# Chunked delta-rule layer on one core: an array cleared on GpSimd, and inverse and merge steps placed ahead of the convolution taps in VectorE's order

## The reference, cut to what matters

```
h = layernorm(x) * (1 + ca) + sa                      # ca, sa, ga: rows of silu(c) @ wmod
q, k = silu(conv4(h @ Wq)), silu(conv4(h @ Wk))       # conv4: causal, 4 taps along the sequence
v = silu(conv4(h @ Wv));  gate = h @ Wg
beta = sigmoid(h @ Wb);   g = -exp(A_log) * softplus(h @ Wa + dt_bias)
S = S * exp(g_t);  S = S + k_t (beta_t (v_t - k_t S));  o_t = q_t S      # for every t, k and q of length 1
x = x + ga * ((rmsnorm(o) * norm_weight * silu(gate)) @ Wo)
x = x + gb * ffn(layernorm(x) * (1 + cb) + sb)
```

## Time and profile before

| | us |
|---|---|
| median of 3 runs | 1088.68 |
| lowest, highest | 1088.04, 1089.65 |
| the profiled execution, its own time | 1088.38 |
| its span, first to last instruction | 1086.3 |
| PE busy | 1043.1 |
| DVE busy | 634.1 |
| ACT busy | 374.6 |
| POOL busy | 208.5 |

### The profile page before, as it was taken

How to read it: one execution, slowest core, us unless ns; L and a number is a source line. 1 busy time by engine, 2 the same in 40 slices (tenths; PEclk the granted TensorE clock), 3 DMA queues, 4 the chain that set the end, 5 groups by cost and what they waited for, 6 DMA issues and landing times.

```text
span 1086.3 us, 18632 instructions
## 1 busy us (share of the span) xinstructions
PE 1043.1 (96%) x7356; PEld 841.0 (77%) x7356; DVE 634.1 (58%) x995; ACT 374.6 (34%) x685; POOL 208.5 (19%) x163
## 2 busy tenths in 40 slices
PE   6999988999998999999899999999999999999998
PEld 4766666878776888888677887888888888888886
DVE  6877357989955777788756233342442433334356
ACT  4576465345446333344463113121121212122110
POOL 1312200011025445444321000000000000004191
PEclk8999998999999999999999999999999999999999
DMA  6505135837447466775630001010010100002223
GB/s 223 181 10 155 40 84 145 246 100 191 93 108 180 103 145 138 176 171 120 218 88 30 1 1 59 1 59 1 18 42 1 59 1 29 30 1 68 78 78 116
DMA packets 153430, 97.34 MB, mean 90 GB/s; under 512 B 93568, under 2 KB 130688, under 8 KB 153216
## 3 DMA queue, kind: packets, MB, share of 16 engines
q1 hardware_dynamic: 153344, 96.16, 32.3%
HBM read 64.67 MB, written 31.46 MB: 88 GB/s over the span
## 4 chain that ended last, share of the span: by engine, by line
PE 80%; DVE 9%; ACT 4%; issue 4%; SPq 1%; DMA 1%; POOL 0%; DVEq 0%; ACTq 0%
PE ps L1277 76%; ACT t L1600 3%; PE ps L1285 3%; DVE t L1976 3%; DVE t L1871 2%; DVE t L1876 1%; PE ps L1483 1%; DMA t<-in_x 1%; DVE t L2087 1%; DVE t L2076 1%; ACT L1622 1%; DVE t L1881 1%; SPq L1214 1%; DMA t<-scrU 0%; DVE t L2042 0%
## 5 line engine op out<-in xcount | busy, mean ns | idle before, releaser
L1277 PE MATMUL ps<-t,t 128*128 128x512 f32 (+6 forms) x6488 | 990.5, 336 | 33.7 <-DVE t L1871 12.2
L1277 PEld LDWEIGHTS ps<-t,t 128*128 128x128 f32 (+4 forms) x6488 | 783.5, 165 | 220.1 <-issue 42.4
L1871 DVE TENSOR_TENSOR t<-ps,t 128x512 f32<-128x512 f32 (+4 forms) x306 | 208.2, 701 | 254.9 <-PE ps L1277 240.2
L1600 ACT ACTIVATE t<-t 128x512 fp32r<-128x512 f32 (+10 forms) x339 | 189.0, 579 | 305.6 <-DVE t L1871 202.3
L1871 DVE TENSOR_TENSOR t<-t,t 128x512 fp32r<-128x512 f32 (+15 forms) x212 | 168.4, 799 | 109.3 <-ACT t L1600 104.9
L1600 ACT ACTIVATE t<-ps 128x512 f32<-128x512 f32 (+5 forms) x202 | 109.2, 552 | 321.0 <-PE ps L1277 309.2
L2355 POOL TENSOR_TENSOR t<-t,t 128x512 f32<-128x512 f32 x16 | 22.5, 1408 | 375.3 <-DVE t L1871 373.1
L1976 DVE SCALAR_TENSOR_TENSOR t<-ps,t,t 128x511 f32<-128x511 f32 (+2 forms) x108 | 80.4, 747 | 21.1 <-ACT t L1600 18.3
L1600 ACT ACTIVATE t<-ps,t 128x512 f32<-128x512 f32 (+2 forms) x93 | 54.6, 618 | 27.4 <-PE ps L1285 11.5
L1285 PE MATMUL ps<-t,t 128*128 128x128 f32 (+1 forms) x388 | 55.4, 276 | 3.9 <-DVE t L1871 1.7
L1285 PEld LDWEIGHTS ps<-t,t 128*128 128x128 f32 (+1 forms) x388 | 42.9, 141 | 14.0 <-issue 5.2
(11 more groups left out here) (50 smaller groups left out, 237.1 us busy)
## 6 DMA issues: line engine op xcount, KB each, us to landing
scrU<-t SPq DMA_DIRECT2D x60, 256.0 KB, 3.0
t<-in_wf SPq DMA_DIRECT2D x16, 768.0 KB, 4.3
t<-scrU SPq DMA_DIRECT2D x32, 288.0 KB, 4.9
t<-scrU SPq DMA_DIRECT2D x32, 192.0 KB, 3.5
t<-in_W SPq DMA_DIRECT2D x19, 256.0 KB, 3.0
t<-in_x SPq DMA_DIRECT2D x16, 256.0 KB, 3.6
t<-in_wmod SPq DMA_DIRECT2D x4, 1024.0 KB, 6.8
t<-in_x SPq DMA_DIRECT2D x32, 128.0 KB, 2.8
```

Source lines behind the costliest of these rows:

```text
L1277: return e.matmul(o, l, r_, start=start, stop=stop, skip_group_check=True)
L1600: return e.activation(o, i, f, **kw)
L1871: return e.tensor_tensor(o, a, b, op)
```

## The change

1. The zero fill of `Pp` (128x3072) moves from DVE to POOL, as a new step `clear_pp`. It waits for the same two semaphores that the DVE fill waited for; DVE's fill of the diagonal waits for POOL's.
2. In a convolution slot with a merge, the first of the slot's two merge steps (`side(0, 1)`) moves from behind the taps to ahead of them, between `put_out` and the taps. (In gate slots it stays where it was.)
3. In convolution slots 8 to 14, while key products are left, lane 0's steps (exponents and key products) move ahead of the taps in the same way.

```
--- before.py
+++ after.py
@@ -542,7 +542,8 @@
 
     def inverse_2():
         yield
-        step("inv2_load")
+        step("clear_pp")
+        step("inv2_load", zeroed=tick("p_pz"))
         for _ in range(4):
             yield
         for i in range(31):
@@ -683,6 +684,10 @@
                 step("conv_in", j=3 + tile, bank=i, done=t, y=y, n=ys["n"], tap=tap)
                 tick("a_conv")
                 put_out()
+                if merging:
+                    side(0, 1)
+                if running[0] and slot > 4 and made["kk"] < 16:
+                    side(0)
                 for k in range(3):
                     step("conv_tap", j=3 + tile, bank=i, y=y, tap=tap, d=k)
                 left[1] = min(left[1], 2)
@@ -693,7 +698,8 @@
             if n == 14:
                 start_b(b)
             if merging:
-                side(0, 1)
+                if tile >= 9:
+                    side(0, 1)
                 plan.append(second)
             for l in (2, 3, 0, 1):
                 side(l)
@@ -2044,10 +2050,7 @@
                                        EI[u % 4][:, :, :].rearrange("p (a m) t -> p a (m t)", a=2), ALU.mult,
                                        ALU.mult).then_inc(sem("v_ab6"), 1)
             elif kind == "inv2_load":
-                e.wait_ge(sem("v_gn"), 10)
-                e.wait_ge(sem("v_turn"), 4)
-                e.memset(Pp[:, :, :, :], 0.0).then_inc(sem("v_fill"), 1)
-                e.wait_ge(sem("v_fill"), 3)
+                e.wait_ge(*at_least(st["zeroed"]))
                 e.memset(Pp[:, :, :, :].rearrange("p i a b -> p i (a b)")[:, :, 0:1024:33], 1.0).then_inc(
                     sem("v_fill"), 1)
             elif kind in ("inv2_mul", "inv2_add"):
@@ -2059,7 +2062,7 @@
                 if kind == "inv2_mul":
                     if i == 0:
                         e.wait_ge(sem("d_nap"), 48)
-                        e.wait_ge(sem("v_fill"), 4)
+                        e.wait_ge(sem("v_fill"), 3)
                         e.wait_ge(sem("k2"), 3)
                     else:
                         e.wait_ge(sem("v_i2a"), i)
@@ -2273,6 +2276,11 @@
                 sh = [128, H, 64]
                 in_order()
                 signal(e.tensor_tensor(IG[u % 8][:, :, :], bc(later, 1, sh), bc(g[:, u, :], 2, sh), ALU.mult), "p_ig")
+            elif kind == "clear_pp":
+                e.wait_ge(sem("v_gn"), 10)
+                e.wait_ge(sem("v_turn"), 4)
+                in_order()
+                signal(e.memset(Pp[:, :, :, :], 0.0), "p_pz")
             elif kind == "clear_p":
                 s = st["s"]
                 if s == 1:
```

## The result

The changed kernel takes 1080.61 us (median of 4 runs, 1079.83 to 1081.82), the kernel before 1089.16 in the runs beside it (1088.04 to 1090.37): ratio 0.9928, 95% interval 0.9917 to 0.994. By the medians that is faster by 8.5 us (the ratio alone stands for 7.8), where 12.9 were forecast; the median lies 1.1 us above the range. The profiled execution took 1079.83 us, its span is 1077.8.

The account below looks back on a forecast made before the run. PE, busy 96% of the span, was taken as the bound, so only its waits for DVE could pay. 4.3 + 3.7 + 2.9 + 2.0 = 12.9 us off gave a forecast of 1075.7 us, 80% range 1073.0 to 1079.5.

Parts of the forecast that it names:

- Key products: Slots 8 to 14: products ahead of taps remove PE's three waits of 1.08, 0.81 and 2.07 us; 4.3 us.
- the three places that the prediction named: Sign in the profile after: exponent matmuls on PE at about 140.7, 144.8 and 154.6 us.
- Fill: Zero fill moved to POOL: PE's waits of 0.23 and 3.24 us up to slot 19 go; 3.7 us.
- So it just holds: Slot 18's taps, behind the first substitution step at 177.5, end at 180; PE wants them in slot 21, at 181.
- tight again: ACT's gate tile, waiting for stores, ends at 204.6; PE asks for its bank in slot 30, at about 205.
- takes 7 us from its first issue to the first step at most: Load of the substitution's blocks back from scrA, from SP's first issue to DVE's first step: at most 7 us.
- The clock: Behind slot 19's 3.24 us wait the granted clock falls to 0.50; without the wait the fall goes, 2.9 us.
- The low bound of 0: Clock term's lower bound: 0 if something else than the wait brings the clock down.
- Merges: First merge step ahead of taps: slot 55's taps run into DVE's later idle time; 2.0 us, bounds 0 and 3.4.
- tight places bind: Rival: PE waits in slots 21 to 31 for taps or gates; gain 10.2 us, 1078.5 us; 14%.
- the one for the clock: Rival: the clock still falls, behind a remaining wait or elsewhere; gain 10.0 us, 1078.7 us; 9%.
- its last two rivals together: Merges give nothing (10%) and the clock still falls (9%), combined: gain 8.0 us, 1080.7 us.

Follow-up runs that it names:

- kernels with four buffers: Changed kernel with four buffers instead of two in `Ab`, the ring of stored products; alone 1077.42 us, ratio 0.9897; four more kernels add further edits.
- the two experiments with the same order: Changed kernel with q's loads three slots later, 1080.77 us; changed kernel with both merge steps ahead of the taps, 1083.3 us.
- one slot later: Substitution's first step one slot later, on the changed kernel with four `Ab` buffers: 1076.83 us; with q's loads later too, 1078.55 and 1076.78 us.
- the four buffers with q's loads later: Changed kernel with four `Ab` buffers and q's tiles read back three slots later; 1079.35 us, ratio 0.9921.

## Why the prediction was wrong

Three of its steps failed, two by what they overlooked and one by what it took for certain.

- **Key products, forecast 4.3 us, measured 2.7** (34.73 to 31.99 us from slot 9 to slot 15 in the changed kernel; 2.55 with this edit alone). The step "so that the key product at 146.98 finds them ready" failed. "A product waits only for its matmuls and exponentials" left out the third condition, the landing of the stores that free its buffer. Before, the taps' 2.31 us stood in front of the products and covered it; with the products first it shows, 1.55 and 1.38 us in the changed kernel. Timeline of DVE there:

```profile
140.57 0.56 DVE L2048 SCALAR_TENSOR_TENSOR t<-ps,t 128x384 f32<-128x384 f32 x1 [1.55 <-DMA scrA<-t]
142.51 0.56 DVE L2048 SCALAR_TENSOR_TENSOR t<-ps,t 128x384 f32<-128x384 f32 x1 [1.38 <-DMA scrA<-t]
142.98 2.31 DVE L1982 SCALAR_TENSOR_TENSOR t<-ps,t,t 128x511 f32<-128x511 f32 x3
```

  Behind it, on ACT, `conv_out` waits for the taps, and the table load and the exponentials stand behind `conv_out`:

```profile
145.38 0.63 ACT L1606 ACTIVATE t<-t 128x512 f32<-128x512 f32 x1 [0.83 <-DVE t L1982]
146.03 1.28 ACT L1628 ACT_TABLE_LOAD   x1
147.32 1.64 ACT L1606 ACTIVATE t<-ps 128x384 f32<-128x384 f32 x4
```

  so PE waits until 148.25. Of the three places that the prediction named, two came where it put them, at 142.04 and 156.01 us (less the late start of 1.66: 140.4 and 154.4, forecast 140.7 and 154.6); the one in the middle, which the text lists among the exponents but is the key product, came at 146.6 by the same count, forecast 144.8. The kernels with four buffers show the cause: there slot 9 to 15 is 29.92 us, 2.07 less than in the changed kernel. Without the landings the term would have been 4.8, more than the 4.3 forecast.

- **Fill, forecast 3.7, measured 3.9** from slot 15 to slot 19 (14.93 us before, 11.02 in the changed kernel); right. But on its own it gives 2.0 back, since the substitution then waits for its blocks in front of slot 18's taps.

- **"So it just holds" and "tight again": both places bind, a little.** The first substitution step was forecast at 177.5; it comes at 181.78, and DVE waits 2.58 us for it where 2 were forecast. Two errors are in that. The chain was to be 8 us earlier: the last product ends at 169.61 (173.06 before), 3.4 earlier, or 5.1 with the late start of slot 9 taken out; the same store landings (1.20 us in front of it) and the 1.6 us by which the products' term fell short are nearly all of the difference. And "takes 7 us from its first issue to the first step at most" was read off one trace in which taps hid the landing: over the eleven executions in which DVE stood waiting for the blocks it was 6.9 to 8.6 us. The rows of the DMA queue and of DVE, changed kernel:

```profile
173.46 2.47 SPq L1170 DMA_DIRECT2D t<-scrA  x3
```

```profile
181.78 0.26 DVE L1877 TENSOR_TENSOR t<-t,t 128x93 f32<-128x93 f32 x1 [2.58 <-DMA t<-scrA]
```

  At slots 21 to 23 PE then loses 0.6 us against an unbroken row in the first profiled execution, 0.9 in the second, 1.8 and 1.5 in the two experiments with the same order, and 0.5 more at the gates in the first alone. The forecast had all of this at nothing; it was 1.1 us in the first profiled execution, 0.1 of which the kernel before loses there too.

- **The clock, forecast 2.9; in the median no sign of a gain.** "The drop and the wait stand together in the trace" was true of one trace. Set against that one execution the term came true: 18 to 24 is 22.83 us with the fall and 19.98 without, 2.85 less. But in three profiled executions up to there (the kernel before twice, the merges alone once) the clock fell in slot 19 once. The forecast took the luck of one execution as a property of the kernel, set it against an execution whose time was the median's all the same, and so counted it as gain.

  Over the fourteen executions thirteen waits of 1.9 to 3.3 us stand between slots 9 and 24, and six of them were followed by a fall, which costs 1.3 to 1.7 us for 3.4 us of half clock and 2.8 to 2.9 for 6.8. The kernel before has two such waits, the changed one has one; at six in thirteen and 1.6 us each that one is worth 0.7 us, an estimate worked out from these counts. The changed order of the merges takes it back, by an estimate of the same kind: it makes one merge wait of 1.2 us, where the longest before is 0.9, and behind it the clock fell in two of the six executions whose wait there was 1.2 us, for 1.3 and 2.8 us, again about 0.7 a run; behind 0.9 it fell in none of four.

  The runs' times can't resolve either estimate, but the record shows no gain: the mean granted clock, which counts falls anywhere in a run, is 0.9927 over 56 executions of the kernel before and 0.9927 over ten of the changed one, where one fall of 6.8 us fewer in each run would make it 0.003 higher. The low bound of 0 stood in the text for another reason.

- **Merges, forecast 2.0, measured 1.8**, alone and with the other edits; right in size. That most of the waits for copies go and waits for transposes come (0.54 and 1.20 us in the changed kernel) is in the rows; that the last slots decide wasn't tested.

The sum in place of 12.9: 2.7 + 3.9 + 1.8, less 1.0 for the tight places and with nothing for the clock, is 7.4 us. The result says 8.5 by the medians and 7.8 by the ratio; the second timing of the changed kernel, 1081.1 against 1088.35, says 7.3, and without any fall of the clock the stretches give 6.7 to 8.0 (9 to 18 and 46 to 58 from executions without a star: 3.13 + 1.78; 18 to 24 from 19.47 or 19.98 to 16.92 or 17.18: 2.3 to 3.1; 24 to 46: 0 to 0.5 lost). The rival "tight places bind" named the right place with a price of 2.7 where it was 1.0; no rival held the store landings, and the one for the clock had 9%, where its price was the forecast's largest error. That its last two rivals together gave 1080.7, almost the measured time, is luck: one of them, merges that give nothing, didn't happen.

## What to carry to other kernels

Before an instruction is moved ahead of another, list all that it waits for, the buffer that it writes among it: a ring's release by a store's landing is invisible in a trace in which something else runs until then. A loss that stands once in one execution, such as a fall of the clock, is a term only at the share of executions in which it occurs; a second profiled execution of the kernel before would have shown it here. And an instruction that will wait for a transfer belongs behind the work that others need, not in front of it: one slot later freed 1.6 to 2.0 us in its stretch, while a merge wait grew from 1.2 to 1.9 us; the times of these runs don't show the gain by itself.

## What the runs showed of the hardware

- The clock falls behind some waits and not behind others of the same length at the same place: 2.07 us before the same twenty matmuls was followed by 1.00 in two executions and by 0.50 or near it in two. The Trainium skill, "TensorE: Matmul & The Clock Gate", section "HAM oscillation — how this bites in real kernels", has the rate return to half behind the waits for DMAs of a thin matmul kernel, in every turn of its loop; the prediction carried that over to this wait. These traces agree for six waits of 1.9 to 3.3 us and not for seven, and the measurement decides: a wait is where a fall can come, not where it must.
- When the clock first rises differs from one execution to the next, and moves all that follows. Fourteen executions with the same instructions on PE reach slot 9 within 133.70 to 136.10 us. The trace's first record of a clock of 1.00 begins at 8.2 to 9.1 us in three of them (the kernel before, the four buffers, and the four buffers with q's loads later) and at 14.0 to 27.1 us in the other eleven. PE's rows show it: the same eight matmuls take 1.02 or 1.03 us in the three and 1.84 in the eleven, here in the kernel before and in the changed one.

```profile
9.38 1.03 PE L1277 MATMUL ps<-t,t 128*128 128x4 f32 x8 [0.88 <-DVE t L1911]
```

```profile
9.28 1.84 PE L1283 MATMUL ps<-t,t 128*128 128x4 f32 x8 [0.88 <-DVE t L1917]
```

  The three reach slot 9 at 133.70 to 134.03 us, the eleven at 134.70 to 136.10. What decides when the clock rises isn't shown.
- The two fills of 3072 columns on GpSimd and VectorE take the same time, 2.66 and 2.62 us, and in the changed kernel VectorE idled 5.78 us (for ACT) over most of the one on GpSimd; its instruction at 135.17, under the fill's last half microsecond, took 0.69 us, as before. The later fills of `P` on GpSimd ran beside VectorE's two-operand instructions of the substitution, and neither was slower: in the kernel before one of 128x525 took 0.71 us beside a fill and 0.71 away from it, and the fills took 2.67 us. For the copies and casts of which the prediction cites the Trainium skill, "SBUF — State Buffer", section "Who interferes with whom", no run here shows whether they and GpSimd can disturb each other.
